# Row loads and stores of attention issued from ScalarE's queue, and one more tile prepared ahead, in a two-layer graph attention kernel

## The reference

```
proj = x @ W[l];  Wh, Ws = split(proj, 2)        # 512 x 1024 weights
a    = softmax(Wh @ Ws.T) * adj
x    = leaky_relu(a @ Wh + x, 0.01)              # l = 0, 1
```

## Time and profile before

| | |
|---|---|
| median of three runs | 2148.17 us |
| profiled execution | 2151.31 us, its span 2149.4 us |
| PE busy | 2110.1 us, 98% of the span |
| DVE busy | 1592.3 us, 74% |
| ACT busy | 908.2 us, 42% |
| POOL busy | 689.5 us, 32% |
| HBM read and written | 123 GB/s over the span |
| queue of SP (q1) | 341.89 MB |
| queue of ACT (q10) | 13.63 MB |

### The profile page before, as it was taken

How to read it: one execution, slowest core, us unless ns; L and a number is a source line. 1 busy time by engine, 2 the same in 40 slices (tenths; PEclk the granted TensorE clock), 3 DMA queues, 4 the chain that set the end, 5 groups by cost and what they waited for, 6 DMA issues and landing times.

```text
span 2149.4 us, 38691 instructions
## 1 busy us (share of the span) xinstructions
PE 2110.1 (98%) x13260; PEld 1295.3 (60%) x13260; DVE 1592.3 (74%) x4057; ACT 908.2 (42%) x2047; POOL 689.5 (32%) x623
## 2 busy tenths in 40 slices
PE   6999999999999999999999999999999999999998
PEld 2456666666666666664446666666666666665444
DVE  7987877788877778876986776776677776767465
ACT  5764344444444444443765344344434443443000
POOL 2853223232223233222863232333323332322000
PEclk9999999999999999999999999999999999999999
DMA  7998878788878687769998987888878978779794
GB/s 216 213 222 155 175 154 164 157 155 161 169 151 166 154 165 159 161 138 236 204 211 183 184 162 165 162 167 172 168 155 171 169 161 181 158 157 220 218 304 133
DMA packets 779526, 380.18 MB, mean 177 GB/s; under 512 B 642880, under 2 KB 701376, under 8 KB 777664
## 3 DMA queue, kind: packets, MB, share of 16 engines
q1 hardware_dynamic: 768512, 341.89, 73.8%
q0 software_dynamic: 3328, 22.16, 7.0%
q10 hardware_dynamic: 7488, 13.63, 1.8%
HBM read 206.24 MB, written 59.11 MB: 123 GB/s over the span
## 4 chain that ended last, share of the span: by engine, by line
PE 91%; DVE 3%; DMA 2%; issue 1%; ACT 1%; SPq 1%; POOL 0%; DVEq 0%; ACTq 0%; POOLq 0%
PE banks L1157 38%; PE banks L1126 31%; PE banks L783 10%; PE banks L1661 7%; PE banks L1135 3%; DMA adj_rows_a<-adj_rows 1%; PE banks L1115 1%; PE banks L605 1%; DVE halves_a L1385 1%; DMA values<-x_rows 0%; DMA probs_t_a<-halves_a 0%; DVE row_a L1340 0%; SPq L1002 0%; DVE adj_low L1453 0%; DVE w_p L725 0%
## 5 line engine op out<-in xcount | busy, mean ns | idle before, releaser
L1157 PE MATMUL banks<-values,probs_t_a 128*128 128x512 f16 x4056 | 961.2, 380 | 7.3 <-DMA probs_t_a<-halves_a 4.2
L1323 POOL TENSOR_TENSOR row_a<-row_a,adj_rows_a 128x512 f32<-128x512 f32 (+1 forms) x364 | 456.7, 1269 | 1163.7 <-ACT row_a L1245 1133.6
L1157 PEld LDWEIGHTS banks<-values,probs_t_a 128*128 128x128 f16 x4056 | 397.3, 98 | 382.2 <-issue 9.6
L1237 ACT ACTIVATE row_a<-banks 128x256 f32<-128x256 f32 x468 | 177.3, 379 | 628.6 <-PE banks L1126 609.1
L1126 PE MATMUL banks<-keys_t,q_even_a 128*128 128x256 f16 x3528 | 430.9, 273 | 1.8 <-DVE peaks_a L1340 1.1
L1385 DVE SCALAR_TENSOR_TENSOR halves_a<-row_a,halves_a 128x512 f16<-128x512 f32 (+1 forms) x364 | 272.5, 749 | 192.1 <-ACT halves_a L1260 189.7
L1126 PEld LDWEIGHTS banks<-keys_t,q_even_a 128*128 128x128 f16 x3528 | 343.8, 98 | 102.5 <-DVE peaks_a L1340 4.9
L1126 PE MATMUL banks<-keys_t,q_odd_a 128*128 128x256 f16 x3024 | 370.0, 273 | 4.4 <-DVE peaks_a L1340 1.8
L1245 ACT ACTIVATE row_a<-row_a,shift_a,scales 128x512 f32<-128x512 f32 (+1 forms) x364 | 281.4, 774 | 174.0 <-DVE shift_a L1375 173.9
L1126 PEld LDWEIGHTS banks<-keys_t,q_odd_a 128*128 128x128 f16 x3024 | 294.3, 98 | 92.1 <-DVE peaks_a L1340 6.0
L1407 DVE SCALAR_TENSOR_TENSOR acc_a<-acc_a,factor_a,banks 128x512 f32<-128x512 f32 x312 | 232.8, 746 | 106.1 <-PE banks L1157 99.3
(11 more groups left out here) (131 smaller groups left out, 1482.7 us busy)
## 6 DMA issues: line engine op xcount, KB each, us to landing
adj_rows_a<-adj_rows SPq DMA_DIRECT2D x312, 256.0 KB, 3.2
adj_t<-adj_blocks POOLq DMA_DIRECT2D x104, 208.0 KB, 3.9
keys_t<-adj_t SPq DMA_DIRECT2D x26, 832.0 KB, 7.9
x_rows_a<-x_rows SPq DMA_DIRECT2D x52, 256.0 KB, 3.6
s_rows<-sum_rows_p SPq DMA_DIRECT2D x24, 512.0 KB, 3.1
values<-x_rows SPq DMA_DIRECT2D x13, 512.0 KB, 5.4
adj_rows_a<-adj_rows SPq DMA_DIRECT2D x52, 128.0 KB, 2.7
x_mid<-x_rows_a SPq DMA_DIRECT2D x26, 256.0 KB, 3.4
```

The costliest lines, as they stand in the source:

```text
L1157: last = pe.matmul(out_bank(u), probs_t[:, turned_slot(w), u, ph * tiles + j, :], values[:, 4 * step_of(w) + j, vh, :], start=(j == 0 and ...
L1237: act.activation(quarter(w, u, odd), as_quarter(bank(w, SET_A)), ACT.Copy).then_inc(scores_copied, 1)
L1323: pool.tensor_tensor(piece, piece, adj_rows[:, n % ADJ_RING, 0:width(w)], ALU.mult).then_inc(masked, 1)
```

## The change

Three things are done. In the projection one more tile is prepared ahead: the constant FILL = 5 takes the place of RING = 4 in the loops that make the halves, so tile 4 gets its halves before the eviction scales are ready (in layer 0 inside `scale_layer`, in layer 1 in the windows after the last pair), and the squares of rows 2 and 3 go from VectorE to ScalarE. Second, the row scales of tiles 2 and 3 come before the low halves of W, and tile 2's high half comes between the two sides of W. Third, in attention all of `load_x`, `load_first`, `store`, `store_products`, the two peak DMAs, the gathering of low bits, the loads of x for the next layer, the loads of products and the first eight loads of adj_t16 move from SyncE's program to the end of ScalarE's iteration, with the same waits. SyncE keeps the adjacency pieces, all transposes, the weight pieces and the query sums.

The diff, cut to its core:

```diff
-RING, X_RING = 4, 3
+RING, X_RING, FILL = 4, 3, 5
@@ scale_layer
         dve.reduce_max(facts[:, 5:6], norms2[:], AX_X).then_inc(norm_peak, 1)
+        if layer == 0:
+            x_lo_half(dve, 4)
         dve.wait_ge(norm_all, layer + 1)
@@ project, act_program
             x_hi_half(act, 1)
+            square_rows(2)
+            square_rows(3)
             act.wait_ge(w_scale_ready, layer + 1)
             for side in (0, 1):
                 for c in range(DC):
                     halve_w(c, cols_of(side))
-            x_hi_half(act, 2)
+                if side == 0:
+                    x_hi_half(act, 2)
             square_rows(FIRST)
             x_hi_half(act, 3)
             for t in range(FIRST + 2, T, 2):
                 square_rows(t)
+            x_hi_half(act, 4)
         act.wait_ge(evict_ready, layer + 1)
         for i in range(last_pair):
             for two in (0, 1):
                 copy_rows(act, 2 * i + two, 0)
-                if 2 * i + RING + two < T:
-                    x_hi_half(act, 2 * i + RING + two)
+                if 2 * i + FILL + two < T:
+                    x_hi_half(act, 2 * i + FILL + two)
@@ project, dve_program (its loop over pairs also has FILL for RING)
             scale_w(dve)
+            dve.wait_ge(squared, FIRST)
+            scale_rows(dve, slice(2, FIRST))
             for side in (0, 1):
                 for c in range(DC):
                     lo_w(c, side)
-            square_rows(2)
-            square_rows(3)
-            scale_rows(dve, slice(2, FIRST))
             x_lo_half(dve, 2)
@@ attend, act_program, end of iteration w (the same calls are gone from sp_program)
-            if ahead and w == windows:
-                for t in range(RING):
-                    ahead["x_hi_half"](act, t)
+            if ahead and 0 <= w - windows < FILL:
+                ahead["x_hi_half"](act, w - windows)
+            if 1 <= i <= J and step == 0:
+                load_x(i - 1)
+            if last_layer and 1 <= i <= J and step == 3:
+                load_first(i - 1, 0)
+                load_first(i - 1, 1)
+            for t, u in late_tiles(w, 5, 6) if last_layer else late_tiles(w, 4, 5):
+                store(t)
+            if last_layer:
+                for t, u in late_tiles(w, 7, 8):
+                    if t < binary["made_here"]:
+                        store_products(t)
+            behind = w - (windows - STEPS) - LAG - 1
+            if ahead and 0 <= behind < WIDE:
+                ahead["load_x"](act, 2 * behind)
+                ahead["load_x"](act, 2 * behind + 1)
+            if ahead and piece_windows.get(w - 3, -1) == pieces - 1:
+                ahead["send_w_peak"](act)
+            if ahead and piece_windows.get(w - 5, -1) == pieces - 1:
+                ahead["fetch_w_peaks"](act)
+            if last_layer and w == 5:
+                binary["gather_low_bits"](act)
+            ending = w - (windows - STEPS)
+            if last_layer and 2 <= ending < 5:
+                binary["load_products"](act, ending - 2)
+            elif last_layer and ending in (5, 6, 12, 13):
+                n = (5, 6, 12, 13).index(ending)
+                binary["load_adj16"](act, 2 * n)
+                binary["load_adj16"](act, 2 * n + 1)
@@ attend, dve_program
-                if 0 <= w - windows < RING:
+                if 0 <= w - windows < FILL:
                     ahead["x_lo_half"](dve, w - windows)
```

More of the change, by code:

```diff
@@ L681, in square_rows @@
         def square_rows(t):
-            n = t if t < 2 else 2 + (t - FIRST) // 2
+            n = t if t < FIRST else FIRST + (t - FIRST) // 2
             act.wait_ge(load_sem(t // 2), landed_load(t // 2))
@@ L755, in dve_program @@
                 square_rows(t)
-            dve.wait_ge(squared, 2 + (T - FIRST) // 2)
+            dve.wait_ge(squared, FIRST + (T - FIRST) // 2)
         scale_rows(dve, slice(early, T))
@@ L760, in dve_program @@
             for two in (0, 1):
-                if 2 * i + RING + two < T:
-                    x_lo_half(dve, 2 * i + RING + two)
+                if 2 * i + FILL + two < T:
+                    x_lo_half(dve, 2 * i + FILL + two)
                 if i >= 1:
@@ L1003, in turn_probs @@
                                    halves[:, unit(w, u) % HALF_RING, 0:2 * width(w)]).then_inc(probs_sem(w, u), 16)
[L1005 to L1023, removed]
-            sp.dma_start(rows_out[t * P:(t + 1) * P, :], work[:, t % 2]).then_inc(stored[t % 2], 16)
         def turn_bits(t):
@@ L1048, in sp_program @@
                     load_adj(w + 1, 0)
-            if ahead and piece_windows.get(w - 3, -1) == pieces - 1:
-                ahead["send_w_peak"](sp)
-            if ahead and piece_windows.get(w - 5, -1) == pieces - 1:
-                ahead["fetch_w_peaks"](sp)
-            if last_layer and w == 5:
-                binary["gather_low_bits"](sp)
             if w in piece_windows:
@@ L1072, in sp_program @@
                     turn_queries(sp, i + 1, n)
[L1073 to L1074 removed]
             if last_layer:
[L1076 to L1078 removed]
                 for t, u in late_tiles(w, 5, 6):
[L1080 removed]
                     turn_bits(t)
[L1082 to L1096 removed]
+            else:
+                if 0 <= w - windows < RING:
                     ahead["turn_x"](sp, w - windows)
[L1098 to L1100 removed]
     def sign_bank(t):
@@ L1229, in act_program, with load_x, load_first, store @@
     def act_program(act):
+        def load_x(i):
+            if i == 0:
+                act.wait_ge(values_lo, first_pair + J)
+                act.wait_ge(queries_summed, 2 * (first_pair + J))
+            for u in (0, 1):
+                if last_layer and i >= 1:
+                    act.wait_ge(x_used, used(i, 0))
+                elif first_pair + i >= 1:
+                    act.wait_ge(stored[u], 16 * (first_pair + i))
+                t = 2 * i + u
+                act.dma_start(x_rows[:, u], x_in[t * P:(t + 1) * P, :]).then_inc(row_loaded[u], 16)
+        def load_first(i, u):
+            t = 2 * i + u
+            act.wait_ge(x_used, used(i, u + 1))
+            act.dma_start(x_rows[:, u], x_first[t * P:(t + 1) * P, :]).then_inc(first_loaded[u], 16)
+        def store(t):
+            act.wait_ge(rows_done, layer * T + t + 1)
+            act.dma_start(rows_out[t * P:(t + 1) * P, :], work[:, t % 2]).then_inc(stored[t % 2], 16)
+        def store_products(t):
+            act.wait_ge(products_kept, t + 1)
+            act.dma_start(products_out[t * P:(t + 1) * P, :], product_rows[:, t % 2]).then_inc(products_stored[t % 2], 16)
         def copy_scores(w, n):
@@ L1273, in act_program @@
         for w in range(windows + STEPS + 2):
+            i, step = pair_of(w), step_of(w)
             copy_scores(w, 0)
```

26 lines of the change are left out of this document (removed).

## The result

The changed kernel takes 2188.7 us (median of five runs, 2186.87 to 2193.38), where the kernel before took 2149.87 us beside it: ratio 1.0182, 95% interval 1.0166 to 1.0199. It is slower by about 39 us. The forecast was 2144.5 us and its range ended at 2153. The spans of the two profiled executions are 2185.8 and 2149.4 us, so 36.4 us are to be found.

The account below looks back on a forecast made before the run. The prediction took TensorE's unbroken matmuls to bound the kernel, so moving DMAs could win back only waits. Its terms, +1.0 + 2.5 - 7.2 = -3.7 us from a median of 2148.17, gave 2144.5 us, range 2139.5 to 2153.

Parts of the forecast that it names:

- Queues: Attention DMAs moved to ScalarE: issue time in ordinary pairs hidden behind its wait for TensorE; cost 0, at most 2 us.
- The sign of being wrong that I had named: If score copies make TensorE wait in ordinary pairs, issuing on ScalarE costs more than taken and the forecast is wrong.
- Gains, -7.2 us: Waits won back by the moved queue: 2.5 at layer 0's end, 3.5 at layer 1's end, 1.2 at the peak store.
- The piece at 982 and the turn at 1984: Last-window adjacency piece of layer 0 (6.35 us landing) and late probability turn of layer 1 (7.14 us), both behind bulk loads.
- The gain at the end of layer 1: End of attention in layer 1: TensorE's waits for turned probabilities shrink; between 0 and 4.2 us, taken as 3.5.
- The gain at the end of layer 0: End of attention in layer 0: TensorE's wait behind an accumulation shrinks; between 0 and 3.0 us, taken as 2.5.
- Peak store, -1.2 us: Layer 0's 0.5 KB peak store no longer delays the adjacency piece behind it; gain between 0 and 1.4 us, taken as 1.2.
- Product loads, +2.5 us: Last pair of layer 1: ScalarE's issue of product loads delays score copies in three windows; +2.5 us, bounds 0 and +6.
- Start, +1.0 us: Layer 0's start: tile 4's low half before the eviction scales delays tile 6's turn; +1.0 us, bounds 0 and +1.5.
- Deeper fill, 0: Projection loops with FILL = 5: the new ring takes 9.96 us per pair against TensorE's 10.38, so cost 0.
- the ring binds the projections: Rival, chance 0.12: turns landing in 5.0 us make the projection's ring 11.3 us per pair, adding 16.6 us; 2161 us.
- The rival that went by it: Rival, chance 0.20: the second queue does not help, small pieces land as late as before, only costs remain; 2151.7 us.

Follow-up runs that it names:

- e1: The changed kernel with load_first issued by SyncE again at its old place; 2170.86 us, ratio 1.0096 to the kernel before.
- f3: The kernel before, all on SyncE, with the second pair of adj_t16 loads one window later; ratio 0.9971, 6.2 us faster.
- e3: The kernel before with only the bulk loads (next layer's x, products, adj_t16) moved to ScalarE's queue; 2159.62 us, ratio 1.0044.
- e9: The changed kernel with only load_first issued one window later, still on ScalarE's queue; 2171.69 us, ratio 1.0077 to the kernel before.
- e11: The kernel before with only the 22 loads of kept products moved to ScalarE's queue; ratio 1.0009.
- f2: The kernel before, all on SyncE, with tile 6's turn of x ahead of the turns of pair 0's keys in layer 0; ratio 0.9988.
- e5: The kernel before with only load_first moved to ScalarE's queue, issued in step 3; ratio 1.0037.
- e12: The kernel before with only the eight big loads of adj_t16 at the end of layer 1 moved to ScalarE's queue; ratio 1.0004.
- e7: The kernel before with only load_first moved to ScalarE's queue and issued one window later; ratio 0.9992.

## Why the prediction was wrong

The step that failed is in "Queues": the moved DMAs were costed by ScalarE's issue time alone, "Cost 0, upper bound 2 us in all". The issue time was right (0.40 us) and hidden, but each moved DMA also moved in time. On SyncE `load_first` stood behind the pieces and turns of its window; on ScalarE it was issued ahead of them. I had checked what waits behind the moved instruction on the engine it goes to, and what it frees on the one it leaves, and not what it will now run beside. That is 14.1 us in the ordinary pairs of layer 1, and 18.5 us of the run by `e1`. The sign of being wrong that I had named came, score copies that TensorE waits for in ordinary pairs, but not for the reason that I gave with it, the cost of issuing.

- **Gains, -7.2 us: none arrived.** "The piece at 982 and the turn at 1984 no longer stand behind them, though the bytes still use the same engines": the half-sentence behind the comma was the truth. In the changed kernel three of the last turns of layer 1 land in 8.8 to 10.4 us. TensorE's wait for turned probabilities went down by 2.6 us, and that for accumulations up by 6.8. The change of layers cost 9.4 us instead of giving 2.5. The gain at the end of layer 1 existed (`f3`, 6.2 us, more than the 3.5 I took, since I had left out the 1.7 us at the lower clock behind the wait), but by moving the bytes in time. The gain at the end of layer 0 was too large to begin with, read from one profile.
- **Peak store, -1.2 us: not there.** At its place the changed kernel waits 2.6 us, not 1.40. The forecast blamed the queue, because 0.5 KB are "no load on the engines". The traces say otherwise. Before, the two row loads issued right behind the store were late too (9.5 and 9.8 us), and the core moved 35 GB/s with its DMA engines 67% busy:

```profile
480.00:484.00 4.00, 4.00 (x26) 2.35 (x24) 2.71 (x7) 1.91 (x4) 1.81 (x3) 1.00 0.67 35
```

  In the changed kernel, with the store on ScalarE's queue at 479.9, it took 11.4 us, a turn that SyncE had issued 0.6 us ahead of it 12.2 us, and the piece behind them 11.0 us. So everything in flight there is slow, whichever queue it is in. No run leaves out or moves the peak store alone, and whether it is the cause stays open.
- **Product loads, +2.5 us: right for the changed kernel.** TensorE loses 2.8 us in these three windows (0.64, 1.38 and 0.78), at some 0.65 us a load. In the profiles of `e1`, `e3` and `e9` it is 1.3 to 1.7 us and in that of `e11`, alone, 0.7; by the ratio `e11` has +1.9 us (-0.2 to +3.9).
- **Start, +1.0 us: not seen.** Tile 6 starts at 54.64 instead of 54.81; in twelve other kernels with the old start it is 54.1 to 56.9. The order on SyncE that I named as its limit was the limit (`f2`). But the 2.4 us read as waiting for tile 6 were 0.53 us of waiting; the rest was tiles 4 and 5 running slowly (the granted clock was 0.76 from 40 to 47). In `e5`, with the same code there and the clock up, TensorE waits 2.56 us, and tile 6 starts at 54.78.
- **Deeper fill, 0: wrong, +3.9 us.** That the ring (9.96 us per pair) doesn't bind TensorE (10.38) was right: the projection ran on unbroken. But the turns of x and keys had been ahead of TensorE, and that lead is what attention starts from: TensorE idles 1.8 to 2.0 us longer there in all four kernels with the deeper fill. The rival "the ring binds the projections" had the wrong mechanism and 0.12 of the chances, and its 16.6 us did not come.
- **The rule that spoke against it.** The Trainium skill, "DMA: Bandwidth & Descriptors", section "Issuing engines are not separate DMA queues", says that DMAs from any engine share the same 16 DMA engines and that only issue time is saved. The runs agree that nothing is gained: `e12`, with only the adj_t16 loads moved, has 1.0004, and the changed kernel still has turns of 8.8 to 10.4 us there. The rival that went by it had 0.20, but it ended at 2151.7 us. Neither it nor the rule has turns and pieces that get later than they were, and that is what `load_first` and the loads of x cost. The other reading, that transfers in a queue of their own are spared by bulk in another, fails in the traces: in `e12` two turns and a piece, issued from 1970.36 to 1972.43 beside the first two adj_t16 loads in ScalarE's queue, land in 7.7 to 9.7 us; before, the turn behind these two loads in the one queue took 7.9.

No rival I wrote had this mechanism: a transfer that nobody waits for, issued beside one that TensorE waits for. That the bytes of the moved loads could delay others more than before was given no price at all, so the chances had nothing above 2161 us.

## What to carry to other kernels

A hand-written order on one queue is also a priority list. Before a DMA goes to another engine's queue, look at what is in flight at the time at which it would be issued there, and who waits for that. A move to a free moment (`e7`, `f3`) was free or gained; a move to another queue at a busy moment cost 7.9 us for 22 loads alone, and 18.5 us with the other rows and the bulk in that queue too. And a ring that keeps pace still costs something if it used to run ahead and a later stage starts from its last output.

## What the runs showed of the hardware

Turns land late with bytes beside them. A turn of probabilities landed in 2.4 us ahead of the moved adj_t16 loads (`f3`), in 3.6 to 4.3 us in the median of layer 1, and in up to 10.9 us beside row loads, a cast and a turn of queries. The first turn of x in layer 1 went from 4.14 to 11.1 us beside 512 KB loads. TensorE's longer stops were often followed by a short stretch at the lower level of the granted clock (1.2 instead of 2.4 GHz): in the changed kernel at 158.8, 500.2, 1001.9, 1015.6 and 2012.3, behind stops of 2.57, 2.62, 4.56, 4.50 and 4.31 us, which adds 1.7 us to each stall. In ten kernels with the same code up to there, TensorE is 0.8 to 6.1 us later at 970 us than in the kernel before, so a difference of a few us at one place of one profile says little without a second kernel that has the same code there.
